# One output run of two rows, x's products in two 64x128 tiles, and M in eight 64x32 tiles

## The chip, the cores and the metric

The kernel runs on one core of a Trainium2 chip. The metric is the device time of one execution in microseconds. A core has the engines TensorE (PE), VectorE (DVE), ScalarE (ACT), GpSimd (POOL) and SyncE (SP), and 16 DMA engines. TensorE multiplies a loaded (stationary) matrix by a streamed (moving) one into PSUM, 8 banks of 512 fp32 numbers on each of 128 partitions; its array can be used as smaller tiles, each on its own rows and columns. SBUF is the working memory of 128 partitions.

## The reference

x has shape (128, 64, 512): 128 batches, 64 channels c, 512 times t. Each batch b has a subject s (one of 8 matrices W0, 64x64) and a condition (one of 200 matrices W1, 64x64).

```
x = x + einsum('bct,bcd->bdt', x, W0[subject])
x = x + einsum('bct,bcd->bdt', x, W1[condition])
```

All in fp32. Both steps together are one product: with M[b] = (I + W0[subject]) (I + W1[condition]), the output is M[b] transposed times x[b]. Input x and the output are 16.8 MB each; the gathered W1 matrices are 2.1 MB.

## The kernel before, in words

The kernel forms M for every batch and applies it to x once.

**Loads.** SP loads the conditions, then x in 16 DMAs of 1 MB (L110). A partition of `xy` holds, for one batch, two adjacent channels (j = 0, 1), 4 KB in a run; a slot is 4 batches, so a partition's row is (batch, channel pair). POOL builds the identity and, as soon as the conditions are there, issues one indirect DMA (L130) that gathers W1 of every batch, one batch in a partition. ACT loads W0 and the subjects.

**Preparation.** DVE clears `w0t_diag` in two parts, the second once the gather has been issued. PE turns W0 (L159), DVE adds the identity and writes `w0t`, twice, on either half of the partitions (L269). When the gather has landed DVE adds 1 to W1's diagonals (L276), and PE turns W1 in 8 turns of 8 transposes each (L171): 128x64 in, 64x128 out. DVE and ACT copy turns 0, 2, 4, 6 and 1, 3, 5, 7 from PSUM to `w1`, in two copies of 64x512 a turn (L222).

**Products that make M.** The 64 pairs of batches go in 8 groups of 8 pairs (16 batches, 4 slots). POOL picks the subject's matrix by a register and copies it into one of the two diagonal blocks of a 128x128 matrix of `w0t_diag` (L151, 16 copies a group). PE multiplies it by the pair's `w1` (L183), and DVE and ACT copy the group's M to `m`, four copies of 32x256 each (L236).

**x's products.** For a unit v (2 slots, 8 batches, 1 MB of x) PE makes 16 matmuls of 32x64 (L202): four row tiles (a batch each) by two column tiles (the slot), twice (the channel j), 512 columns each. Four banks hold a unit's result; there are six. DVE copies one slot's four pieces of 64x512 and ACT the other's (L242), over x in `xy`. Then SP writes the unit (L116): a partition holds one channel of a batch, so a run is 2 KB.

**Order.** It is written out by hand, each engine in its own list. PE: products of group g+1, then x's products of group g. DVE and ACT: copies of group g's x products, then the M copies of group g+2. SP: all loads, then the 16 outputs, each after its unit's eight copies.

Times name a matmul in fp32 as two records (two passes); a transpose is one. In the text a product is one instruction of the program.

Of the kernel before, what the change touches and what calls it, by code (L numbers as in the profile page):

```python
# [5 lines left out]
def bass_cond_residual_kernel(  # L6
# [15 lines left out]

    fp32 = mybir.dt.float32
# [5 lines left out]
    P = 2 * C  # L29
    J = 2  # L30
    Q = C // J
    PAIRS = B // 2
    SLOT = 4
    SLOTS = B // SLOT
    GROUP = 4
    GROUPS = SLOTS // GROUP
    GPAIRS = 2 * GROUP
    CHUNK = 2
    CHUNKS = SLOTS // CHUNK
    assert CHUNK == 2  # L40
    BANK = 512
    assert B == P and T == BANK and GPAIRS * C == BANK
    ROWS = S0 * C // P
    D_RING = 4
    M_RING = 2
    M_BANK = 6
    Y_BANKS = 6
    TURN = 8
    TURNS = C // TURN
    W1_RING = 3  # L50
    POOL = mybir.EngineType.Pool
    HALVES = [slice(0, C), slice(C, P)]

    x_view = x_dram.rearrange("(s b) (p j) t -> (b p) s (j t)", b=SLOT, j=J)
    out_view = out_dram.rearrange("(p h) c t -> (h c) p t", h=2)

    ctx = ExitStack()
    with ctx:  # L58
# [10 lines left out]
        w1 = sb("w1", [P, PAIRS, C], fp32)  # L69
        w0t_diag = sb("w0t_diag", [P, D_RING, GPAIRS, P], fp32)  # L70
        m = sb("m", [P, M_RING, GROUP, J, C], fp32)
# [11 lines left out]
        s_gather_sent = sem("s_gather_sent")  # L83
        s_zeros = sem("s_zeros")
        s_ident = sem("s_ident")
        s_d_clear = sem("s_d_clear")
# [6 lines left out]
        s_w0_diag = sem("s_w0_diag")  # L93
# [6 lines left out]
        s_x = [sem(f"s_x{n}") for n in range(CHUNKS)]  # L100
        s_out = [sem(f"s_out{n}") for n in range(CHUNKS)]

        block = ctx.enter_context(nc.Block())

        @block.sync
        def _(sp):
            sp.dma_start(cond[:, :], cond_dram.rearrange("(b o) -> b o", o=1)).then_inc(s_cond, 16)
            for n in range(CHUNKS):
                slots = slice(n * CHUNK, (n + 1) * CHUNK)
                sp.dma_start(xy[:, slots, :], x_view[:, slots, :]).then_inc(s_x[n], 16)  # L110
            for n in range(CHUNKS):

                sp.wait_ge(s_y_v, SLOT * (n + 1))
                sp.wait_ge(s_y_s, SLOT * (n + 1))
                pairs = slice(n * 2 * CHUNK, (n + 1) * 2 * CHUNK)
                sp.dma_start(out_view[:, pairs, :],  # L116
                             xy[:, n * CHUNK:(n + 1) * CHUNK, :].rearrange("q s (h t) -> q (s h) t", h=2)
                             ).then_inc(s_out[n], 16)
            for n in range(CHUNKS):
                sp.wait_ge(s_out[n], 16)  # L120

        @block.gpsimd
        def _(pool):
# [12 lines left out]
            pool.wait_ge(s_ident, 1)  # L136
            pool.wait_ge(s_gather, 16)
            pool.wait_ge(s_subjects, 16)
            pool.wait_ge(s_d_clear, 2)
            pool.wait_ge(s_w0t, 4)  # L140
            for g in range(GROUPS):
                if g >= D_RING:

                    pool.wait_ge(s_m_psum, g - D_RING + 1)
                first = g * 2 * GPAIRS
                _, picked = nc.values_load_multi_w_load_instructions(
                    subjects[0:1, first:first + 2 * GPAIRS], engines=(POOL,), min_val=0, max_val=S0 - 1,
                    skip_runtime_bounds_check_because="subjects index the 8 matrices")
                for n in range(2 * GPAIRS):
                    h, rows = n % 2, HALVES[n % 2]  # L150
                    nc.gpsimd.tensor_copy(w0t_diag[rows, g % D_RING, n // 2, h * C:(h + 1) * C],  # L151
                                          w0t[rows, bass.ds(picked[n] * C, C)]).then_inc(s_w0_diag, 1)

        @block.tensor
        def _(pe):
# [6 lines left out]

            pe.wait_ge(s_w1_plus, 1)
            for n in range(TURNS):
# [4 lines left out]
                for z in range(TURN):  # L169
                    bank = 2 * (n % W1_RING) + z // 4  # L170
# [4 lines left out]
            def products(g):  # L175

                pe.wait_ge(s_w0_diag, 2 * GPAIRS * (g + 1))
                if g >= M_RING:

                    pe.wait_ge(s_m_v, 4 * (g - M_RING + 1))  # L180
                    pe.wait_ge(s_m_s, 4 * (g - M_RING + 1))
# [4 lines left out]
                last.then_inc(s_m_psum, 1)  # L186

            def apply(g):

                pe.wait_ge(s_m_v, 4 * (g + 1))  # L190
                pe.wait_ge(s_m_s, 4 * (g + 1))
                for v in range(g * GROUP // 2, (g + 1) * GROUP // 2):
                    pe.wait_ge(s_x[v], 16)
                    for j in range(J):
                        for r in range(SLOT):
                            rows = slice(r * Q, (r + 1) * Q)
                            if j == 0 and SLOT * v + r >= Y_BANKS:

# [12 lines left out]
            for g in range(GROUPS):  # L211
                if g + 1 < GROUPS:
                    products(g + 1)
                apply(g)
# [96 lines left out]
```

## Time and profile before

| | |
|---|---|
| median of 3 runs | 99.78 us (99.7 to 100.39) |
| profiled execution | 100.29 us, of which the span 97.4 us |
| busy PE / PE loads / DVE / ACT / POOL | 69.0 / 37.3 / 67.6 / 54.8 / 31.8 us |
| busy mean of the 16 DMA engines | 98% or more until 75 us, 50 to 90% after |
| moved | 35.9 MB, 19.0 MB read, 16.8 MB written |

The span is what the trace covers; the rest of the execution's time, 2.9 us, lies around it. PE and PE loads overlap, and matmuls in different tiles overlap too, so that busy time says less of PE than the pace of its records.

### The profile page before, as it was taken

Reading aid. Unit: us, or ns where it says so; the run is one execution under the profiler, and the core shown is the slowest. Engines: PE = TensorE matmul, PEld = TensorE weight load, DVE = VectorE, ACT = ScalarE, POOL = GpSimd, SP = SyncE. Lnnn points to the kernel's source line nnn. Section 1 sums busy time; section 2 is a strip of 40 time slices with the busy share of each in tenths; the row PEclk is TensorE's granted clock in tenths of the full one; section 3 lists DMA queues with packets and bytes.
Section 4 is the critical chain, followed back from the end, with each engine's and each line's share of the span. In section 5 each row is a group of like instructions: output and inputs, shape, how many; then the busy total and the mean of one; then the engine's idle time right before and its main releaser. Section 6 shows DMA issues by size and latency. Waiting matters only on the chain.

```text
span 97.4 us, 2078 instructions
## 1 busy us (share of the span) xinstructions
PE 69.0 (71%) x708; PEld 37.3 (38%) x708; DVE 67.6 (69%) x111; ACT 54.8 (56%) x105; POOL 31.8 (33%) x135
## 2 busy tenths in 40 slices
PE   0400007997799999699699699979969969998000
PEld 0200006996782382265147138236414613322000
DVE  4293000588088889979979988997997997977900
ACT  2200000356277689759939938965992993955800
POOL 2400001888788788787758300000000000000000
PEclk9999999999999999999999999999999999999965
DMA  1999999999999999999999999999998984877975
GB/s 25 339 416 453 422 412 410 410 407 416 405 409 405 410 407 409 409 407 405 407 405 408 372 407 410 405 410 406 401 407 346 391 303 167 314 274 274 380 278 203
DMA packets 13243, 35.90 MB, mean 369 GB/s; under 512 B 689, under 2 KB 818, under 8 KB 13106
## 3 DMA queue, kind: packets, MB, share of 16 engines
q1 hardware_dynamic: 12944, 33.56, 88.5%
q0 software_dynamic: 144, 2.10, 5.0%
q10 hardware_dynamic: 146, 0.13, 0.4%
q8 instruction: 5, 0.08, 0.3%
q14 instruction: 4, 0.03, 0.1%
HBM read 19.01 MB, written 16.78 MB: 367 GB/s over the span
## 4 chain that ended last, share of the span: by engine, by line
PE 37%; DVE 34%; DMA 14%; issue 8%; DVEq 1%
PE psum L202 28%; DVE xy L242 21%; DVE m L236 12%; DMA w_rows<-in_L_cond_weights_dram,cond 12%; PE psum L171 8%; DMA cond<-in_itok_B_dram 3%; PE psum L183 2%; DVE w L222 1%; DVEq L58 1%; DVE w_rows L276 0%
## 5 line engine op out<-in xcount | busy, mean ns | idle before, releaser
L242 DVE COPY xy<-psum 64x512 f32<-64x512 f32 x64 | 43.8, 684 | 7.5 <-PE psum L202 5.8
L202 PE MATMUL psum<-xy,m 32*64 32x512 f32 x512 | 44.6, 600 | 5.1 <-DVE xy L242 5.1
L242 ACT COPY xy<-psum 64x512 f32<-64x512 f32 x64 | 37.2, 582 | 15.2 <-PE psum L202 13.8
L151 POOL COPY w0t_diag<-w0t 64x64 f32 x128 | 30.0, 234 | 19.9 <-issue 12.6
L202 PEld LDWEIGHTS psum<-xy,m 32*64 32x64 f32 x512 | 14.2, 130 | 29.9 <-DVE xy L242 18.4
L183 PEld LDWEIGHTS psum<-w,w0t_diag 128*128 128x128 f32 x128 | 14.8, 192 | 6.4 <-POOL w0t_diag L151 2.4
L183 PE MATMUL psum<-w,w0t_diag 128*128 128x64 f32 x128 | 15.7, 277 | 1.3 <-DVE w L222 1.3
L171 PE MATMUL psum<-ident,w_rows 128*64 128x128 f32 x64 | 8.5, 301 | 10.7 <-DVE w_rows L276 10.7
L236 DVE COPY m<-psum 32x256 f32<-32x256 f32 x32 | 13.3, 416 | 3.7 <-PE psum L183 2.8
L222 ACT COPY w<-psum 64x512 f32<-64x512 f32 x8 | 4.6, 578 | 17.3 <-PE psum L171 17.3
L236 ACT COPY m<-psum 32x256 f32<-32x256 f32 x32 | 11.7, 365 | 3.1 <-PE psum L183 2.4
L171 PEld LDWEIGHTS psum<-ident,w_rows 128*64 128x64 f32 x64 | 7.8, 155 | 11.7 <-DVE w_rows L276 11.2
L222 DVE COPY w<-psum 64x512 f32<-64x512 f32 x8 | 5.5, 683 | 3.6 <-PE psum L171 3.6
L276 DVE TENSOR_SCALAR w_rows<-w_rows 128x64 f32<-128x64 f32 x1 | 0.2, 225 | 6.7 <-DMA w_rows<-in_L_cond_weights_dram,cond 6.7
L159 PE MATMUL psum<-ident,w_rows 128*64 128x128 f32 x4 | 1.0, 414 | 3.5 <-DMA w_rows<-in_L_cond_weights_dram 3.5
L260 DVE MEMSET w0t_diag<- 128x2048 f32 x1 | 1.8, 1765 | 2.1 <-DMA w_rows<-in_L_cond_weights_dram,cond 2.1
L258 DVE MEMSET w0t_diag<- 128x2048 f32 x1 | 1.8, 1765 | 1.2 <-PEq L298 1.2
L222 ACT ACT_TABLE_LOAD x1 | 1.3, 1283 | 1.8 <-issue 1.8
L159 PEld LDWEIGHTS psum<-ident,w_rows 128*64 128x64 f32 x4 | 0.5, 157 | 3.6 <-issue 3.5
L130 POOL DMA_INDIRECT w_rows<-in_L_cond_weights_dram,cond x1 | 1.1, 1120 | 2.0 <-DMA cond<-in_itok_B_dram 2.0
L269 DVE TENSOR_TENSOR w0t<-psum,ident 64x256 f32<-64x256 f32 x4 | 1.4, 395 | 0.0
L126 POOL TENSOR_SCALAR_AFFINE_SELECT ident<-ident 128x128 f32<-128x128 f32 x1 | 0.3, 288 | 0.2 <-POOL ident L124 0.2
(5 smaller groups left out, 0.6 us busy)
## 6 DMA issues: line engine op xcount, KB each, us to landing
xy<-in_x_dram SPq DMA_DIRECT2D x16, 1024.0 KB, 19.5
out_dram<-xy SPq DMA_DIRECT2D x16, 1024.0 KB, 8.6
w_rows<-in_L_cond_weights_dram ACTq DMA_DIRECT2D x1, 128.0 KB, 2.6
cond<-in_itok_B_dram SPq DMA_DIRECT2D x1, 0.5 KB, 2.5
subjects<-in_itok_B_dram ACTq DMA_DIRECT2D x1, 0.5 KB
w_rows<-in_L_cond_weights_dram,cond POOLq DMA_INDIRECT x1, 11.5
```

The source lines that it names most:

```text
L130: nc.gpsimd.indirect_dma_start(out=w1_rows[:, :, :].rearrange("b d e -> b (d e)"), out_offset=None, in_=w1_dram.rearrange("s d e -> s (d e)"),
L151: nc.gpsimd.tensor_copy(w0t_diag[rows, g % D_RING, n // 2, h * C:(h + 1) * C], w0t[rows, bass.ds(picked[n] * C, C)]).then_inc(s_w0_diag, 1)
L159: last = nc.tensor.transpose(w0_psum[:, z * P:(z + 1) * P], w0_rows[:, z, :], ident[:, :])
L171: last = nc.tensor.transpose(psum[0:C, bank, (z % 4) * B:(z % 4 + 1) * B], w1_rows[:, :, n * TURN + z], ident[:, :])
L183: last = nc.tensor.matmul(psum[:, M_BANK + g % M_RING, k * C:(k + 1) * C], w0t_diag[:, g % D_RING, k, :], w1[:, g * GPAIRS + k, :], start= ...
L202: last = nc.tensor.matmul(psum[columns, (SLOT * v + r) % Y_BANKS, :], m[rows, g % M_RING, 2 * v + w - g * GROUP, j, :], xy[rows, 2 * v + w ...
L222: last = copy(w1[rows, :, n * TURN:(n + 1) * TURN], turned[:, h, :, :])
L236: copy(m[quarter, g % M_RING, :, j, :], of[:, a, :, :]).then_inc(done, 1)
L242: copy(xy[HALVES[r % 2], 2 * v + w, (r // 2) * T:(r // 2 + 1) * T], psum[HALVES[w], (SLOT * v + r) % Y_BANKS, :]).then_inc(done, 1)
L258: nc.vector.memset(w0t_diag[:, 0:2, :, :], 0.0).then_inc(s_d_clear, 1)
L260: nc.vector.memset(w0t_diag[:, 2:4, :, :], 0.0).then_inc(s_d_clear, 1)
L269: nc.vector.tensor_tensor(w0t[rows, :].rearrange("q (s j k y) -> q j s k y", s=S0, j=J, y=J)[:, j, :, :, :], turned[:, j, :, :, :], one[:, ...
```

## The change

- A slot's output is made in two 64x128 tiles: PE takes the rows of two batches (64 partitions) at once, and `m_diag` holds their M in a block-diagonal 64x128 stationary matrix whose other half is zero. A slot is 4 products of 512 columns, two for each of its two banks (L217), so a unit is 8 in place of 16. The even and the odd output channels come out in the two halves of the partitions and are copied so that `xy` holds two adjacent channels, 4 KB, in a run again, and `out_view` writes them so. A unit is still 2 slots, 1 MB.
- PSUM: three slots of two banks are in flight in place of six single banks, and a slot's copies are two for each of DVE and ACT (four in all, 64x512 as before).
- M: POOL (for the first two units DVE) copies the picked W0 matrix without a diagonal, `w0b`; PE makes M in 64x32 tiles, 16 products a unit (two row tiles, four column tiles, twice), in place of 4 a unit of 128x128.
- W1 is turned by matmuls with every other four columns of the identity, in two column tiles of 128x64: 128 products of 64 columns in place of 64 transposes of 128. A turn fills one bank and is copied in one copy of 128x512.
- The blocks of M are 1, 1, 2, 2, 2, 4 and 4 units. M's copies of a block go to `m_diag`, four an engine, of 32 x 128 numbers for each unit of the block.
- SP loads three slots of x, waits until the gather has been issued, and then loads the rest.
- DVE clears `m_diag` (128x4096) once, after the gather has been issued.

```diff
+    BLOCKS = [(0, 1), (1, 1), (2, 2), (4, 2), (6, 2), (8, 4), (12, 4)]
+    Y_RING = 3
-    out_view = out_dram.rearrange("(p h) c t -> (h c) p t", h=2)
+    out_view = out_dram.rearrange("(s b) (q i) t -> (b q) s (i t)", b=SLOT, i=J)
...
+            load(0, 2)
+            load(2, 1)
+
+            sp.wait_ge(s_gather_sent, 1)
+            load(3, 1)
+            for v in range(2, UNITS):
+                load(2 * v, 2)
...
-                    last = nc.tensor.transpose(psum[0:C, bank, (z % 4) * B:(z % 4 + 1) * B],
-                                               w1_rows[:, :, n * TURN + z], ident[:, :])
+                    for odd, rows in enumerate(HALVES):
+                        last = nc.tensor.matmul(psum[rows, n % W1_RING, z * C:(z + 1) * C],
+                                                w1_rows[:, :, n * TURN + z], of[:, odd, :, :],
+                                                start=True, stop=True)
...
-                for k in range(GPAIRS):
-                    last = nc.tensor.matmul(psum[:, M_BANK + g % M_RING, k * C:(k + 1) * C],
-                                            w0t_diag[:, g % D_RING, k, :], w1[:, g * GPAIRS + k, :],
-                                            start=True, stop=True)
+                if k >= 1:
+                    pe.wait_ge(s_m_v, SLOT * k)
+                    pe.wait_ge(s_m_s, SLOT * k)
+                for v in range(first, first + n):
+                    for j in range(J):
+                        for r in range(SLOT):
+                            for odd, rows in enumerate(HALVES):
+                                at = (v % M_COLUMNS * J + j) * C
+                                last = nc.tensor.matmul(psum[QUARTERS[r], M_BANK + odd, at:at + C],
+                                                        w0b[rows, v * SLOT + r, j * Q:(j + 1) * Q],
+                                                        w1[rows, v * SLOT + r, :], start=True, stop=True)
...
-                            for w, columns in enumerate(HALVES):
-                                last = nc.tensor.matmul(psum[columns, (SLOT * v + r) % Y_BANKS, :],
-                                                        m[rows, g % M_RING, 2 * v + w - g * GROUP, j, :],
-                                                        xy[rows, 2 * v + w, j * T:(j + 1) * T],
-                                                        start=j == 0, stop=j == J - 1)
+                    if s >= Y_RING:
+
+                        pe.wait_ge(s_y_v, 2 * (s - Y_RING + 1))
+                        pe.wait_ge(s_y_s, 2 * (s - Y_RING + 1))
+                    for j in range(J):
+                        for h, rows in enumerate(HALVES):
+                            last = nc.tensor.matmul(psum[:, 2 * (s % Y_RING) + h, :],
+                                                    m_diag[rows, odd, v % M_RING, j, :],
+                                                    xy[rows, s, j * T:(j + 1) * T],
+                                                    start=j == 0, stop=j == J - 1)
...
+            for n in range(EARLY * UNIT):
+                v, odd, r = n // UNIT, n // SLOT % 2, n % SLOT
+                nc.vector.tensor_copy(w0b[HALVES[odd], v * SLOT + r, :],
+                                      w0t[HALVES[odd], bass.ds(picked[n] * C, C)]).then_inc(s_w0b_early, 1)
```

PE's list before, from the turning of W1 through the first groups (`psum<-xy,m` are x's products, `psum<-w,w0t_diag` those that make M, each row's count at its end):

```order
L171 MATMUL psum<-ident,w_rows 64x128 x64
L183 MATMUL psum<-w,w0t_diag 128x64 x16
L202 MATMUL psum<-xy,m 64x512 x32
L183 MATMUL psum<-w,w0t_diag 128x64 x8
L202 MATMUL psum<-xy,m 64x512 x32
```

And the same place of PE's list in the changed kernel, with the last blocks:

```order
L178 MATMUL psum<-ident,w_rows 64x64 x128
L198 MATMUL psum<-w,w0b 32x64 x32
L217 MATMUL psum<-xy,m_diag 128x512 x8
L198 MATMUL psum<-w,w0b 32x64 x32
L217 MATMUL psum<-xy,m_diag 128x512 x8
```

Two units (a group of before) took 8 products for M and 32 for x; they take 32 for M and 16 for x now, and x's first products come after two blocks of 16.

DVE's list at the start, before:

```order
L258 MEMSET w0t_diag 128x2048
L260 MEMSET w0t_diag 128x2048
L269 TENSOR_TENSOR w0t<-psum,ident 64x8x32 x4
L276 TENSOR_SCALAR w_rows<-w_rows 128x64
L222 COPY w<-psum 64x64x8 x8
L236 COPY m<-psum 32x4x64 x8
```

and now, where the pair of an address instruction (ISA) and a copy comes 16 times before W1's diagonal (L300):

```order
L274 MEMSET m_diag 128x4096
L284 TENSOR_TENSOR w0t<-psum,ident 64x8x32 x4
L289 TENSOR_LOAD subjects
L295 ISA
L295 COPY w0b<-w0t 64x64
```

The addition to W1's diagonals, on which the turning of W1 waits, has moved behind these copies and behind the whole of the clearing.

## Rows read from the trace of the kernel before

**Rows 1.** The page, 40 slices, in tenths: PEclk granted clock, DMA busy share.

```profile
PEclk9999999999999999999999999999999999999965
DMA  1999999999999999999999999999998984877975
```

**Rows 2.** Chain of waits (start us, us, what), 84 us to the end.

```profile
83.63 2.67 PE psum L202 x26
...
87.06 2.67 PE psum L202 x24
...
89.75 0.68 DVE xy L242
```

**Rows 3.** Source view of the output DMAs, L116.

```profile
L116 SPq DMA_DIRECT2D out_dram<-xy x16: 372/373/4838, 33.8 to 92.6; - x16
...
DMA to landing us min/median/max: 4.3/8.6/19.4
```

**Rows 4.** Windows: one group of two units.

```profile
core 0: us, PE busy (x) PEld busy (x) DVE busy (x) ACT busy (x) POOL busy (x), PEclk, DMA share, GB/s
44.30:52.37 8.07, 7.30 (x81) 3.56 (x80) 7.12 (x13) 6.12 (x12) 5.93 (x26) 1.00 1.03 405
```

**Rows 5.** Timeline of PE loads (start us, us), first steps of L202.

```profile
28.89 0.24 PEld L202 LDWEIGHTS psum<-xy,m 32*64 32x64 f32 x16 [0.20 <-DVE m L236]
29.37 0.18 PEld L202 LDWEIGHTS psum<-xy,m 32*64 32x64 f32 x8 [0.25 <-issue]
```

**Rows 6.** Windows (span, busy PE, busy PE loads) on L183, products for M.

```profile
25.00:26.82 1.82, 1.75 (x16) 1.78 (x16) 1.00 1.02 405
```

**Rows 7.** Windows (columns of Rows 6) on L171, early and later turns of W1.

```profile
15.20:17.20 2.00, 1.94 (x10) 1.60 (x10) 1.00 1.03 414
18.90:19.78 0.88, 0.88 (x10) 0.88 (x9) 1.00 1.01 405
```

**Rows 8.** Windows (span, busy PE loads) just after a wait had ended.

```profile
85.07:85.11 0.04, 0.04 (x2) 1.00 1.24 461
```

**Rows 9.** Timeline of PE (start us, us) where L202 and L183 take turns.

```profile
42.37 2.00 PE L183 MATMUL psum<-w,w0t_diag 128*128 128x64 f32 x16
44.30 1.11 PE L202 MATMUL psum<-xy,m 32*64 32x512 f32 x16
```

**Rows 10.** Page, groups: line, engine, out<-in, count, busy, mean ns, idle before.

```profile
L242 DVE COPY xy<-psum 64x512 f32<-64x512 f32 x64 | 43.8, 684 | 7.5 <-PE psum L202 5.8
...
L236 DVE COPY m<-psum 32x256 f32<-32x256 f32 x32 | 13.3, 416 | 3.7 <-PE psum L183 2.8
...
L269 DVE TENSOR_TENSOR w0t<-psum,ident 64x256 f32<-64x256 f32 x4 | 1.4, 395 | 0.0
```

**Rows 11.** Chain of waits, start to the first x product.

```profile
3.49 11.46 DMA w_rows<-in_L_cond_weights_dram,cond
...
15.26 7.65 PE psum L171 x56
...
25.07 1.98 PE psum L183 x16
...
28.89 2.80 PE psum L202 x40
```

**Rows 12.** Timeline, the second clearing and the last ACT copies of W1.

```profile
5.10 1.76 DVE L260 MEMSET w0t_diag<- 128x2048 f32 x1 [2.10 <-DMA w_rows<-in_L_cond_weights_dram,cond]
...
23.80 1.17 ACT L222 COPY w<-psum 64x512 f32<-64x512 f32 x2 [0.58 <-PE psum L171]
```

**Rows 13.** DMA queues between 7.8 and 14.4 us (q0 is the gather).

```profile
q0 software_dynamic: 143, 2.10, 74.2%
q1 hardware_dynamic: 193, 0.73, 26.8%
```

**Rows 14.** Source view of POOL copies, L151 (ns min/median/max, first and last start).

```profile
L151 POOL COPY w0t_diag<-w0t x128: 230/236/245, 16.5 to 54.3; 64x64 f32 x128
```

**Rows 15.** DMA over a stretch of writes, 50 to 72 us.

```profile
DMA packets 4443, 8.86 MB, mean 403 GB/s; under 512 B 135, under 2 KB 135, under 8 KB 4439
```

More of the change, by code:

```diff
@@ L188, in apply, with products @@
[L188 to L193, printed above, removed]
+            def products(k):
+                first, n = BLOCKS[k]
+                if first + n <= EARLY:
+                    pe.wait_ge(s_w0b_early, UNIT * (first + n))
+                else:
+                    pe.wait_ge(s_w0b, UNIT * (first + n - EARLY))
+                if k >= 1:
+                    pe.wait_ge(s_m_v, SLOT * k)
+                    pe.wait_ge(s_m_s, SLOT * k)
+                for v in range(first, first + n):
@@ new lines, in products, with apply @@
+                last.then_inc(s_m_psum, 1)
+            def apply(k):
+                first, n = BLOCKS[k]
+                pe.wait_ge(s_m_v, SLOT * (k + 1))
+                pe.wait_ge(s_m_s, SLOT * (k + 1))
+                for s in range(2 * first, 2 * (first + n)):
+                    v, odd = s // 2, s % 2
+                    pe.wait_ge(s_x[v], 32 if v == 1 else 16)
+                    if s >= Y_RING:
[7 more added lines that the diff above has]
+                                                    start=j == 0, stop=j == J - 1)
@@ L210, in _ @@
             products(0)
[L211 to L214, printed above, removed]
+            for k in range(len(BLOCKS)):
+                if k + 1 < len(BLOCKS):
+                    products(k + 1)
+                apply(k)
         def copy_w1(eng, copy, done, n):
             eng.wait_ge(s_w1_turned, n + 1)
-            bank = 2 * (n % W1_RING)
-            turned = psum[0:C, bank:bank + 2, :].rearrange("q z (k p h) -> q h p (z k)", h=2, k=4)
@@ L238, in copy_y @@
[L238 to L254 removed]
+            part = slice(n * TURN // J, (n + 1) * TURN // J)
@@ new lines, in copy_w1, with copy_m @@
+            copy(w1[:, :, :].rearrange("q p (i e) -> q p i e", i=J)[:, :, :, part],
+                 psum[:, n % W1_RING, :].rearrange("q (y i p) -> q p i y", i=J, p=UNITS * SLOT)).then_inc(done, 1)
+        def copy_m(eng, copy, done, odd, k):
+            first, n = BLOCKS[k]
+            eng.wait_ge(s_m_psum, k + 1)
+            if first + n > M_RING:
+                eng.wait_ge(s_y_psum, 2 * (first + n - M_RING))
+            at = first % M_COLUMNS * J * C
+            for r, rows in enumerate(QUARTERS):
+                to = m_diag[rows, odd, first % M_RING:first % M_RING + n, :, :].rearrange(
+                    "q v j (i b e) -> q b (v j) i e", i=J, b=2)
+                copy(to[:, r % 2, :, :, :],
+                     psum[rows, M_BANK + odd, at:at + n * J * C].rearrange("q (w i e) -> q w i e", i=J, e=Q)
+                     ).then_inc(done, 1)
@@ new lines, in copy_y, with copies @@
+        def copy_y(eng, copy, done, i, s):
+            eng.wait_ge(s_y_psum, s + 1)
+            for h, rows in enumerate(HALVES):
+                copy(xy[rows, s, i * T:(i + 1) * T], psum[HALVES[i], 2 * (s % Y_RING) + h, :]).then_inc(done, 1)
+        def copies(eng, copy, w1_done, m_done, y_done, odd):
+            for n in range(odd, TURNS, 2):
+                copy_w1(eng, copy, w1_done, n)
+            eng.wait_ge(s_m_clear, 1)
+            copy_m(eng, copy, m_done, odd, 0)
+            copy_m(eng, copy, m_done, odd, 1)
+            for k, (first, n) in enumerate(BLOCKS):
+                for s in range(2 * first, 2 * (first + n)):
+                    copy_y(eng, copy, y_done, odd, s)
+                if k + 2 < len(BLOCKS):
+                    copy_m(eng, copy, m_done, odd, k + 2)
```

124 lines of the change are left out of this document (41 added, 83 removed).

## The prediction

> **What bounds the kernel now.** I read the page's slices first [rows 1]: the DMA engines are full until about 75 us and no longer, and PE's granted clock is full (2.4 GHz) until the last x product. So the last quarter is set by the engines, and the chain of waits there says by which [rows 2]: units follow each other every 3.43 us (83.63, 87.06) where no M is made, PE 2.67 us of it and one DVE copy. The last unit's copies start at 89.75, DVE's four take 2.83 us (each 0.684 and a gap of 0.03 [rows 10]), the last output is issued at 92.6 and lands after 4.3 us [rows 3]. From the last copy's end (92.58) to the span's end are 4.8 us. A group of two units with its products takes 8.07 us [rows 4], 4.04 a unit: DVE is busy 7.12 of it, so it is nearly as close to the bound as PE.
>
> How PE works is in the loads' timeline [rows 5]: eight tiles load and start together, and the next step follows after 0.43 to 0.48 us (28.89, 29.37). I take 0.429 us for 512 columns in one tile, in one pass of two; 16 products are 32 records in 8 tiles, four steps, 1.72 us of array for a unit. Four steps and a wait for copies in six banks make 3.43. The products for M cost 16 records in 1.82 us [rows 6], 0.112 each, and a group's 16 records with both changes of tile shape 1.93 us (42.37 to 44.30 [rows 9]).
>
> Before all that lies the gather: issued 3.49, landed 14.95, W1 turned from 15.26, products from 25.07, x's products from 28.89 [rows 11].
>
> **The change, part by part.** The sum follows PE from the gather on.
>
> *Gather.* While it moved its 2.10 MB, x took 0.73 MB of the same DMA engines [rows 13], at 0.41 MB/us 1.8 us. Now only 1.5 MB of x are queued before; but SP's next load is issued the moment the gather's issue is known (5.10, when DVE's second clearing starts [rows 12]), and from there x competes as before. Bounds: 0 and 1.8 us earlier; I take 0.6, near the low end, as x's three slots fill the queue until about 6.8 us and the rest follows at once. Landing 14.35.
>
> *DVE before it.* From 5.10: clearing 2 x 1.76 [rows 12], W0 1.46 for four, with its gap, then 16 picked copies of 64x64. A copy of 512 columns costs 0.684 and of 256 0.416 [rows 10], so 64 give 0.215, with a gap of 0.033 0.25; POOL's follow each other at 0.30 with all its gaps ((54.3 - 16.5) / 127 [rows 14]). 16 x 0.25 = 4.0: ready at 14.1, just under the gather. The cover is thin: at POOL's pace it is 14.9. Then the diagonal, 0.25: PE starts at 14.65 in place of 15.26.
>
> *Turning W1.* Before, a turn was 8 transposes of 128 columns at 0.109 (0.88 [rows 7]), the first 2.6 us at half that pace (10 records in 2.00 us [rows 7]) although the clock row shows full clock. Now it is 32 records of 64 columns in two column tiles, 16 a tile. A load of 64 columns is half of row 6's 0.112, a matmul of 64 half of 0.109; overlapped, 0.056 a record, 0.90 a turn, if the two tiles run side by side as eight do in [rows 5]. 8 x 0.90 + 1.3 for the slow start + 0.2 = 8.7 (8.5 before). If they do not, 15.9. ACT's last copies were 1.17 us in two [rows 12] and are one of 0.58. The products for M start at 14.65 + 8.7 + 0.03 + 0.58 + 0.07 = 24.0, 1.0 us earlier.
>
> *The first block.* The price of a small product is the main unknown. 16 products of a unit are 32 records in 8 tiles, 4 a tile at 0.056: 0.22 us of array. So what counts is how fast PE is fed. Nearest row: after a wait had ended, two products' loads start within 0.04 us [rows 8]; I take 0.036 each, 0.58 a unit. Lower bound the array, 0.014; upper bound the transposes' 0.109. 24.0 + 0.58 + 0.28 until the copies can start, four copies of 32x128 at 0.282 and 0.033 (1.26), then the second block's 0.58 and 0.25 to change: x's products start at 26.95. Block 1 waits for block 0's copies because both lie in the same two banks; that wait is in this sum.
> The Trainium skill, TensorE: Matmul & The Clock Gate, section Wait — 56ns, not 53.3ns?, says that a matmul costs about 62 ns of the sequencer's time when the hardware does not decode it, which binds for small ones. By it the sum would come to 104.7 in place of 99.1; the row shows two in 0.04 us and speaks for less.
>
> *x's products.* 8 products a unit, 16 records, but only two tiles of 64x128: 8 steps of 0.429, 3.43 us a unit where the array took 1.72. The other half of each stationary matrix is zero, so this is twice the array time for the same output. It is new on the path in full, and it takes the place of waits: three slots of two banks let PE run 5.1 us ahead of a copy, and a slot's two DVE copies take 1.43. Even behind M's copies for a block of four units (4 x 0.72 = 2.9) the bank comes free in time. 16 x 3.43 = 54.9 us.
>
> *Products for M, blocks 2 to 6.* 14 units, 224 products; 8 of each of the five blocks I count as queued behind x's products and free (16 loads start within 0.23 us in [rows 5]). 184 x 0.036 = 6.6, and 5 changes there and back at 0.35 (1.93 less 16 x 0.112 gives 0.14 from first product to x; with the step before it I take 0.35): 8.4 us. Per unit in the middle 3.43 + 0.6 = 4.0, as before; DVE's 2.87 + 0.9 = 3.8 lies just beneath it, and POOL's 16 copies for two units (16 x 0.30 = 4.8 [rows 14]) under both.
>
> *End.* 26.95 + 54.9 + 8.4 + 0.16 = 90.4. Only one slot is then to be copied: 0.03 + 1.43 in place of 2.83, 91.85. With 4.8 the span is 96.65, against 97.4. The 4 KB runs cost nothing and give nothing: writes in 2 KB runs moved 403 GB/s [rows 15] with the engines full, and from 75 us on they wait for outputs.
>
> The profiled execution had 100.29 with this span, 2.9 around it; the sum gives 99.55. The median is 0.5 lower: **99.1 us**. A measurement of this kernel can tell about 1% (98.8 to 100.8), so the forecast is no change, at its fast edge.
>
> **Rivals.**
> *Slow feeding, on the other side.* If a small matmul is issued at 0.055, half the transposes' 0.109 (each of those is a load and a matmul), the 216 products on the path (184 and the first two blocks' 32) cost 0.019 x 216 = 4.1 us more: 103.2. For it: no row shows a long stream of small ones, and 8 in flight would soon be used up. Against it: [rows 8]. It decides at 0.044 each, where the time passes 100.8.
> *Array pace.* If PE takes them as fast as queued loads start in [rows 5] (0.015), M's products cost 0.24 a unit: 3.9 us less over 184, 0.7 in the first blocks; DVE's 3.8 a unit then holds back about 1 us of it: 95.5. An earlier gather, up to 1.2 us, only counts if DVE's copies are faster too.
> *Column tiles one after the other* in W1's turning: 7.2 us more, 106. [rows 5] speak against it.
> *DVE's early copies late*, or no gain of the gather: 0.6 to 1 us more, 99.7 to 100.1.
> *The DMA engines as bound:* 15 outputs behind 19 MB of reads would end near 88, before the last unit; out.
>
> **Chances.** As forecast, within 1.2 us: 0.36 (faster by over 1% 0.15, within 1% 0.20, slower 0.01). Array pace: 0.24, faster. Slow feeding: 0.25 (slower 0.24, same 0.01). Column tiles: 0.08, slower. Late DVE: 0.07 (same 0.05, slower 0.02). In all faster 0.39, same 0.26, slower 0.35. Both signs hold most of it, so the forecast's own range is 97.9 to 100.3; the range for 8 in 10 is 95.2 to 104.2, from the array pace to slow feeding with a little more.
>
> **What would show it.** x's products: 16 records a unit at 0.21 us, 3.43 a unit, PE without waits. Products for M: two units within 1.1 us by my price, 0.5 by the array's, 1.8 by slow feeding. Turns of W1 every 0.90 us, not 1.8. Gather landing at 14.0 to 14.6 and DVE's last picked copy just before. One slot's copies after the last matmul. Wrong it is if DVE, not PE, ends the steps, or if two 64x128 tiles do not run together (then x's products alone would take 110 us).

## The result and the profile after

| | before | after |
|---|---|---|
| median | 100.09 us (99.7 to 104.27, 4 runs) | 107.63 us (107.07 to 108.14, 4 runs) |
| profiled execution, span | 100.29, 97.4 us | 107.07, 105.3 us |
| a turn of W1 (of 8), once under way | 0.88 us | 2.34 us |

The ratio is 1.0766 [1.0664, 1.0868]: slower by 7.7%, and outside the predicted range, which ended at 104.2. The ratio leaves out the one execution of 104.27 us of the kernel before, a slow one.

The chain of waits of the changed kernel (start us, us, what) answers to [rows 2, 11]:

```profile
3.46 10.29 DMA w_rows<-in_L_cond_weights_dram,cond
...
14.05 18.95 PE psum L178 x252
33.00 0.72 issue
33.73 0.55 PE psum L198 x29
...
35.71 0.68 PE psum L198 x32
36.39 4.90 PE psum L217 x16
41.29 0.79 PE psum L198 x53
42.08 3.63 PE psum L217 x16
...
71.39 27.69 PE psum L217 x128
99.08 0.02 issue
99.11 0.68 DVE xy L257
```

From 36.39 us to the last copy PE has the chain alone: every wait for DVE in the middle of the kernel has gone, as predicted. (The chain counts the records that it followed, x252; the kernel has 256 of them.) But L178, the turning of W1, has the chain for 18.95 us, where L171 had it for 7.65.

Laid side by side with [rows 2, 11], the stretches add up to the 7.9 us by which the span grew:

| stretch | before | after | difference |
|---|---|---|---|
| span's start to the turning | 15.26 | 14.05 | -1.21 |
| turning to the first product for M | 9.81 | 19.68 | **+9.87** |
| to the first x product | 3.82 | 2.66 | -1.16 |
| to PE's end (a copy follows at 89.75 and at 99.11) | 60.84 | 62.69 | +1.85 |
| to the span's end | 7.67 | 6.22 | -1.45 |

Windows on L178 (span, busy PE with records, busy loads with records, granted clock, DMA share, GB/s), the answer to [rows 7]: the first, the second and the last turn.

```profile
14.05:16.40 2.35, 2.35 (x32) 2.35 (x34) 1.00 1.03 422
16.40:18.74 2.34, 2.34 (x36) 2.34 (x36) 1.00 1.03 411
30.44:32.78 2.34, 2.34 (x36) 2.34 (x34) 1.00 1.03 406
```

A turn is 32 records, 16 in each column tile, and takes 2.34 us: 0.146 for a pair, or 0.073 a record. The pace is the same in the first turn as in the last, no wait is named, and in the last the clock is full (for the first see below). So this is not a slow start, and not a missing cover: it is a steady price of a record itself, its load and its matmul together. The page's group of these loads (busy us, mean ns, idle before) says which of the two to suspect:

```profile
L178 PEld LDWEIGHTS psum<-ident,w_rows 128*64 128x64 f32 x256 | 18.8, 251 | 10.0 <-DVE w_rows L300 10.0
```

One load of 64 columns is shown with 251 ns, 3.4 times as long as its share of the time, so more than one is open all the time. Loads overlap matmuls in a record, however, and a long load may only be one that waits. That has to be tried.

The small products and the clock, windows again (the first on L198, the others on all of PE):

```profile
41.29:42.08 0.79, 0.79 (x64) 0.63 (x64) 1.00 1.05 410
```

```profile
35.00:36.00 1.00, 0.29 (x24) 0.75 1.03 406
36.00:37.00 1.00, 1.00 (x33) 0.50 0.99 397
...
38.00:39.00 1.00, 1.00 (x6) 0.54 1.06 414
39.00:40.00 1.00, 1.00 (x8) 1.00 0.99 393
```

32 products for M (64 records) take 0.79 us, 0.025 each. And after 35 us the granted clock falls to 0.50, the lower level of 1.2 GHz, for 3.4 us; in [rows 1] it never fell before the end. x's first unit takes 4.90 us for this, the second 3.63.

One thing about the clock has to be known for all that follows. The trace's own record of the granted clock begins only at 18.43 us here and at 18.01 us in the kernel before; ahead of that the page and the windows print full clock because they have no record, not because it was read. In the kernel before, the pace of L171 changes at just that place: its transposes start every 0.213 us until 17.84 us and every 0.109 us from 18.36 on. L178 keeps 0.073 a record on both sides of 18.43.

### The profile page after: what moved, and what is told of

The parts are those of the page before. It is cut to its first block, busy times and chain, and to the rows that moved or that the text cites. A ratio compares the mean times of both kernels' runs of the same rounds, so it can differ in the third digit from the quotient of the medians.

```text
span 105.3 us, 2665 instructions
## 1 busy us (share of the span) xinstructions
PE 83.8 (80%) x1028; PEld 50.1 (48%) x1028; DVE 66.8 (63%) x118; ACT 51.9 (49%) x97; POOL 23.7 (22%) x119
## 4 chain that ended last, share of the span: by engine, by line
PE 79%; DMA 12%; DVE 2%; issue 1%; DVEq 1%; ACTq 0%; POOLq 0%
PE psum L217 55%; PE psum L178 18%; DMA w_rows<-in_L_cond_weights_dram,cond 10%; PE psum L198 6%; DMA subjects<-in_itok_B_dram 2%; DVE m_diag L249 1%; DVEq L64 1%; DVE xy L257 1%; ACTq L305 0%; DVE w_rows L300 0%; POOLq L149 0%; DVEq L241 0%
## 5 line engine op out<-in xcount | busy, mean ns | idle before, releaser
L217 PE MATMUL psum<-xy,m_diag 64*128 64x512 f32 x256 | 57.8, 604 | 0.0
L217 PEld LDWEIGHTS psum<-xy,m_diag 64*128 64x128 f32 x256 | 25.2, 191 | 28.4 <-issue 27.9
L178 PE MATMUL psum<-ident,w_rows 128*64 128x64 f32 x256 | 18.9, 320 | 9.5 <-DVE w_rows L300 9.5
L157 POOL COPY w0b<-w0t 64x64 f32 x112 | 21.9, 239 | 11.0 <-DMA w_rows<-in_L_cond_weights_dram,cond 9.4
L178 PEld LDWEIGHTS psum<-ident,w_rows 128*64 128x64 f32 x256 | 18.8, 251 | 10.0 <-DVE w_rows L300 10.0
L249 DVE COPY m_diag<-psum 32x256 f32<-32x256 f32 (+2 forms) x28 | 12.8, 458 | 4.4 <-PE psum L198 3.6
L249 ACT COPY m_diag<-psum 32x256 f32<-32x256 f32 (+2 forms) x28 | 11.0, 394 | 2.8 <-PE psum L198 2.2
L198 PEld LDWEIGHTS psum<-w,w0b 64*32 64x32 f32 x512 | 5.5, 108 | 6.3 <-issue 6.3
L198 PE MATMUL psum<-w,w0b 64*32 64x64 f32 x512 | 6.7, 230 | 2.2 <-DVE m_diag L249 1.5
L165 PE MATMUL psum<-ident,w_rows 128*64 128x128 f32 x4 | 1.0, 414 | 3.5 <-DMA w_rows<-in_L_cond_weights_dram 3.5
L165 PEld LDWEIGHTS psum<-ident,w_rows 128*64 128x64 f32 x4 | 0.5, 160 | 3.5 <-issue 3.5
L300 DVE TENSOR_SCALAR w_rows<-w_rows 128x64 f32<-128x64 f32 x1 | 0.2, 225 | 1.1 <-DMA w_rows<-in_L_cond_weights_dram,cond 1.1
```

The source lines that it names most:

```text
L157: nc.gpsimd.tensor_copy(w0b[HALVES[odd], v * SLOT + r, :], w0t[HALVES[odd], bass.ds(picked[n] * C, C)]).then_inc(s_w0b, 1)
L165: last = nc.tensor.transpose(w0_psum[:, z * P:(z + 1) * P], w0_rows[:, z, :], ident[:, :])
L178: last = nc.tensor.matmul(psum[rows, n % W1_RING, z * C:(z + 1) * C], w1_rows[:, :, n * TURN + z], of[:, odd, :, :], start=True, stop=True)
L198: last = nc.tensor.matmul(psum[QUARTERS[r], M_BANK + odd, at:at + C], w0b[rows, v * SLOT + r, j * Q:(j + 1) * Q], w1[rows, v * SLOT + r, : ...
L217: last = nc.tensor.matmul(psum[:, 2 * (s % Y_RING) + h, :], m_diag[rows, odd, v % M_RING, j, :], xy[rows, s, j * T:(j + 1) * T], start=j = ...
L249: copy(to[:, r % 2, :, :, :], psum[rows, M_BANK + odd, at:at + n * J * C].rearrange("q (w i e) -> q w i e", i=J, e=Q)).then_inc(done, 1)
```

## The experiments

**Theory L (loads).** The stationary matrix of the turning is `w1_rows[:, :, z]`: of each partition 64 numbers that lie 256 bytes apart. Such a load costs more than 0.056 us, and the two column tiles don't double its pace. Before, the same 64 numbers were loaded once, for a transpose of 128 columns that is one record (0.109), which hid the load. Now they are loaded four times: there are two products of 64 columns, one for each column tile, and a product in fp32 is two records, each with its own load (64 records of L171 have become 256 of L178). **Rivals:** the moving side (every other four columns of the identity) is slow; column tiles simply run one after the other; or the loss is elsewhere and the turning hides it. **Theory G** is about the clock: it falls because PE does little between 33 and 36 us. Where an experiment changes what is multiplied or where it lands, its text says so.

### The turning alone undone (e1), and again on another chip (e12)

```diff
-                    for odd, rows in enumerate(HALVES):
-                        last = nc.tensor.matmul(psum[rows, n % W1_RING, z * C:(z + 1) * C],
-                                                w1_rows[:, :, n * TURN + z], of[:, odd, :, :],
+                    bank = 2 * (n % W1_RING) + z // 4
+                    last = nc.tensor.transpose(psum[0:C, bank, (z % 4) * B:(z % 4 + 1) * B],
+                                               w1_rows[:, :, n * TURN + z], ident[:, :])
```

The copies of a turn are cut into four pieces for each, since the halves come out beside each other again. All else is as in the changed kernel.

> The changed kernel with W1 turned as before: 64 transposes of 128 columns, six banks, copies in pieces. Theory A (all of the loss is the turning of W1, 18.95 us for 256 records against 8.5): the turning takes 8.3 to 8.8 us again, the four-dimensional copies may add up to 1 us at its end, and the span falls from 105.3 by 9 to 10.5 us to 95 to 96.5 us, a little faster than the kernel before. Theory B (part of the loss is in x's products, 62.8 us from the first to the last against 60.8 before): the span stays above 98.

Measured: median 98.86 us (96.49 to 99.85) with 100.36 for the kernel before. The turning took 10.1 us (13.99 to 24.1). In the profiled execution x's first unit was the slow one, as its chain shows, and the clock beside it:

```profile
28.17 6.23 PE psum L216 x16
...
35.19 3.63 PE psum L216 x16
```

```profile
25.00:26.00 1.00, 0.46 (x32) 1.00 1.01 401
26.00:27.00 1.00, 0.00 (x0) 0.77 1.05 422
27.00:28.00 1.00, 0.51 (x32) 0.50 1.02 406
```

The mean granted clocks of the four executions were 0.949, 0.964, 0.948 and 0.995, and the last was the one of 96.49 us. So about 9 us of loss lie in the turning, and 1.6 to 3.4 us are at stake in the clock. The expectation of theory A was nearly right in kind and not in size: the turning took 10.1 us and not 8.3 to 8.8, since the transposes kept their half pace until 19.7 us, where the clock's record begins in this trace, and the span was 98.1. While the granted clock was 0.50 (26.54 to 33.37 us) a step of x's products took 0.85 us, and 0.43 after it: half the clock, half the pace.

> The kernel of e1_turn_back once more, on another chip, for its spread: its four runs had 96.49 at a mean clock of 0.995 and 98.08 to 99.85 at 0.948 to 0.964. Theory G (the low clock after W1's turning costs 1.5 to 3.5 us and comes in most runs): again most runs at 98 to 100 with a mean clock under 0.97, and a profile in which x's first unit takes 5 to 6.3 us. Rival (a disturbed chip that time): 96.3 to 97 in all.

Measured: median **96.81 us** (96.26 to 97.91), the kernel before 99.92 on the same chip; ratio **0.9784 [0.9675, 0.9894]**. Three of the four had a mean clock of 0.994 to 0.996, and the one of 97.91 us had 0.963: the clock seems to have fallen once in four here and three times in four in e1, which is neither theory G's "most runs" nor the rival's "in all". The profiled execution has a span of 94.5 us. Its chain, and PE's windows in the same pause:

```profile
26.70 0.46 PE psum L197 x29
27.16 3.63 PE psum L216 x16
30.79 0.79 PE psum L197 x53
...
60.83 27.69 PE psum L216 x128
88.52 0.02 issue
88.55 0.68 DVE xy L261
```

```profile
25.00:26.00 1.00, 0.17 (x24) 0.01 (x1) 0.58 (x3) 0.61 (x3) 0.94 (x6) 1.00 1.05 418
26.00:27.00 1.00, 0.30 (x32) 0.33 (x32) 0.56 (x2) 0.42 (x2) 0.94 (x7) 1.00 1.06 426
```

(Columns: busy PE, loads, DVE, ACT, POOL, clock.) PE is as idle as in e1, and the clock holds at 1.00. With it held, the kernel with everything but the new turning is 2.9 us shorter in span than the kernel before: x's first product comes 1.7 us earlier (27.16 against 28.89), what follows PE's end is 1.7 us shorter (5.98 against 7.67), and 0.5 of this is lost between (61.36 against 60.84).

### The moving side packed (e2)

```diff
+            nc.gpsimd.tensor_copy(sel[:, :, :].rearrange("q o (v r) -> q o v r", r=SLOT),
+                                  ident[:, :].rearrange("q (v o r) -> q o v r", o=2, r=SLOT)).then_inc(s_sel, 1)
...
-                                                w1_rows[:, :, n * TURN + z], of[:, odd, :, :],
+                                                w1_rows[:, :, n * TURN + z], sel[:, odd, :],
```

> The changed kernel, but the columns of the identity that are streamed lie packed in a tile of their own, 64 in a run in place of 16 runs of 4; the two column tiles and the loads stay as they are. Theory M (the moving operand's short runs set the 0.147 us of a record in each tile): a turn falls from 2.34 to about 0.9 to 1.0 us, the turning to about 8.7, the span to 95 to 97. Theory L (the loads of W1, 64 numbers 256 bytes apart, take 0.073 each and follow each other though the tiles are two): 2.34 a turn, span 105. Theory C (two 128x64 column tiles run one after the other): also 2.34.

Measured: median 108.27 us, ratio 1.0792 [1.0724, 1.0861]. The turning is one row of the chain:

```profile
14.52 18.90 PE psum L183 x256
```

18.90 us against 18.95: the moving side is not the cause, and theory M falls. Theories L and C both expected this.

### The loads packed (e3; W1 isn't turned)

```diff
-                                                w1_rows[:, :, n * TURN + z], of[:, odd, :, :],
+                                                w1_rows[:, n * TURN + z, :], of[:, odd, :, :],
```

The same instructions, but each load reads 64 neighbouring numbers.

> The changed kernel, but PE loads 64 neighbouring numbers of each partition of W1 in place of 64 that lie 256 bytes apart (so the W1 that it multiplies is not the turned one; the work and its order are the same). Theory L: a turn falls from 2.34 to 0.9 to 1.2 us, span about 95 to 97. Theories M and C: 2.34 a turn, span 105.

Measured in one execution: 101.40 us, span 99.6. Windows on L178, one early and two later:

```profile
14.01:16.04 2.03, 2.03 (x38) 2.03 (x40) 1.00 1.02 412
19.45:20.40 0.95, 0.95 (x40) 0.95 (x37) 1.00 1.03 410
20.40:21.33 0.93, 0.93 (x40) 0.93 (x36) 1.00 1.05 405
```

A turn takes 0.93 us from 19.45 us on, 0.058 a pair, where the prediction said 0.90. So the predicted pace was that of packed loads. And for them the two column tiles do run side by side: in one tile a record of 256 columns takes 0.217 us (the fillers of e7 below, six in 1.30), so one of 64 columns takes about 0.054, an estimate in proportion, and here a record starts every 0.029.

Before about 19.2 us a turn took twice that, 0.053 a record; the clock's record begins at 19.31 here. The strided loads of the changed kernel have no such step: 0.073 on both sides of 18.43, and in e4 the same on both sides of 19.02. So their price does not go with whatever halves PE's pace at the start, which fits numbers that are slow to be fetched and not an array that is slow. Why the spacing costs this much no run shows; only two spacings were tried, 4 and 256 bytes.

The span of 99.6 us is above the 95 to 97 that theory L expected. The kernel lost time in a way that no theory had named: PE stood still three times (0.43 us at 23.03, and the two below), and nothing the profile shows released it.

```profile
52.98 1.59 issue
54.57 0.34 PE psum L198 x15
...
62.94 2.30 issue
65.25 0.73 PE psum L198 x42
```

### One column tile at a time (e4)

```diff
-                        last = nc.tensor.matmul(psum[rows, n % W1_RING, z * C:(z + 1) * C],
+                        last = nc.tensor.matmul(psum[HALVES[z // 4], n % W1_RING, ((z % 4) * 2 + odd) * C:((z % 4) * 2 + odd + 1) * C],
```

Eight products in a row go to one column tile, then eight to the other; they land in other places, so M is another one.

> The changed kernel, but the first eight products of a turn go to one column tile and the next eight to the other, in place of alternating (so the pieces of W1 land in other places; the work is the same). Theory M (0.147 us in each tile, tiles side by side): most of a turn is serial now, 4 to 4.7 us a turn, span 118 to 124. Theory L and theory C (a shared path of 0.073 a record): 2.34 a turn, span 105.

Measured in one execution: 110.78 us. Window of one turn on L178:

```profile
17.00:19.86 2.86, 2.86 (x39) 2.86 (x37) 1.00 1.01 405
```

2.86 us for 32 records is 0.089 each with no neighbour to overlap with; by turns they cost 0.073. Had the tiles run fully side by side it would have been half of 0.089. No theory had expected this number (L and C 2.34 a turn, M 4 to 4.7), but it lies far nearer to L and C. The "serial tiles" rival is nearly true of these loads, and only of these.

### The new turning alone, in the kernel before (e6)

```diff
-                    bank = 2 * (n % W1_RING) + z // 4
-                    last = nc.tensor.transpose(psum[0:C, bank, (z % 4) * B:(z % 4 + 1) * B],
-                                               w1_rows[:, :, n * TURN + z], ident[:, :])
+                    for h, rows in enumerate(HALVES):
+                        last = nc.tensor.matmul(psum[rows, n % W1_RING, z * C:(z + 1) * C],
+                                                w1_rows[:, :, n * TURN + z], of[:, h, :],
```

> The kernel before with one part of the change alone: W1 is turned in two column tiles of 128x64 by every other column of the identity, 256 records in place of 64, each with a load of 64 numbers 256 bytes apart; one copy a turn. Theory L (the loads of both tiles share a path, 0.073 each from W1 as it lies): 2.34 us a turn, the turning 18.7 to 19 us, and the time goes from 100.4 up by 9 to 10.5, less about 0.6 for the single copy at the end: 109 to 110.5. Rival (in the changed kernel something else slows it, POOL's picks beside it or the held loads): 1 us or less.

Measured: 108.89 and 109.12 us in the two executions with a clock near 0.98 (two others took 112.85 and 113.37), against 99.93 for the kernel before. From the chain:

```profile
14.97 19.11 PE psum L172 x256
34.80 1.98 PE psum L185 x16
38.61 2.80 PE psum L204 x40
```

x's products start at 38.61 in place of 28.89. This one part costs 9 us alone; the rest of the change gives some of it back.

### Can the clock be held by filler work? (e7)

e1 with three matmuls of 256 columns ahead of each of the first two blocks of M; their results are overwritten.

```diff
+            def fill(bank, n):
+                for _ in range(n):
+                    nc.tensor.matmul(psum[:, bank, 0:4 * C], ident[:, :], w1_rows[:, 0:4, :], start=True, stop=True)
+            fill(M_BANK, 3)
...
+            fill(0, 3)
```

> W1 turned back to transposes as in e1_turn_back, and PE makes three matmuls of 256 columns that nobody reads in each of its two waits before x's first products. Theory G (the granted clock fell to half at 26.2 us because PE had little to do from 24 to 28, and x's first unit took 6.23 us in place of 3.6): the clock stays full, the span is 94.5 to 95.5 in every run, the time 96.3 to 97.3, 3 to 4% under the kernel before. Rival (the clock falls anyway, or the fillers delay the products): 98 to 99.5 as in e1_turn_back.

Measured: median 101.45 us (100.63 to 102.57), ratio 1.0141 [1.0081, 1.0200]. In the profiled execution the clock held, and x's first unit took 3.63 us; the mean clocks of the six lie between 0.965 and 0.995, so it may not have held in each. And the time is 2.6 us above e1's (98.86, on another chip) and 1.4% above the kernel before: neither theory G's 96.3 to 97.3 nor the rival's 98 to 99.5. The chain shows what took it (L225 are the fillers):

```profile
24.32 1.30 PE psum L225 x6
...
28.18 3.63 PE psum L216 x16
31.81 0.76 PE psum L197 x51
32.57 1.17 issue
...
63.27 0.62 PE psum L216
63.90 1.90 issue
65.80 27.75 PE psum L216 x127
```

The two stalls, 3.07 us, are more than the 2.6 us that the held clock saved in x's first unit (6.23 against 3.63). The span is 99.5 us, 1.4 longer than e1's: the rest of it, 0.9 us, lies in the third products and the last eight units, which the stalls interrupt. Both end 2.4 us after a packet of instructions began to move: the trace's list of DMA packets has one of 16 KB on the instruction queue (q8) at 31.28 and one at 63.37, and PE goes on at 33.74 and 65.80.

### Three questions at e7's size (e8, e9, e11), and fewer fillers (e10)

e8 has SP load x at once, as before:

```diff
-            load(2, 1)
-
-            sp.wait_ge(s_gather_sent, 1)
-            load(3, 1)
-            for v in range(2, UNITS):
+            for v in range(UNITS):
```

> e7_filled, but SP issues all loads of x at once, as before the change. Theory H (holding x back brought the gather forward by 1.2 us, from 14.95 to 13.75): the gather lands at 14.7 to 15.1 and the time is 1.0 to 1.3 us above e7_filled. Rival (the gather landed earlier by chance, or DVE's early copies hold the start anyway): within 0.4 us of it.

Measured: 101.66 us (99.62 to 102.59, 10 executions) against e7's 101.45 on the same chip: no loss to be seen in the time, where theory H expected 1.0 to 1.3 us. Three of the ten even took 99.62 to 100.62, less than the shortest of e7's six (100.63). The gather took 11.31 us from its issue, and 11.04 in e7. e7 is the slowest of ten profiled kernels that hold the loads (10.13 to 11.04, mean 10.46); the three that don't have 11.27 to 11.46. So this pair says 0.3 us, all the kernels together 0.9, and e8 alone does not settle it.

e9 writes runs of 2 KB from the same data (the rows land elsewhere):

```diff
-    out_view = out_dram.rearrange("(s b) (q i) t -> (b q) s (i t)", b=SLOT, i=J)
+    out_view = out_dram.rearrange("(p h) c t -> (h c) p t", h=2)
```

> e7_filled, but the output DMAs write runs of 2 KB through the old view of the output (so the rows land in other places; the bytes are the same). My prediction's theory (4 KB runs give nothing, since outputs wait for the engines): within 0.4 us of e7_filled. Rival (2 KB runs are slower by the 3% that their packets show, 0.084 us for 2 KB against 0.163 for 4 KB, and with x's products starting earlier the DMA engines are near their bound): 0.5 to 1.2 us slower.

Measured: 102.11 us (99.41 to 102.97, 4 executions) against e7's 101.45 (100.63 to 102.57). The median is 0.66 us higher, which is the rival's 0.5 to 1.2 and not the "within 0.4", but the spreads lie over each other. In the profiled executions x's first product comes 0.39 us later (28.57 against 28.18), before anything is written, and 0.30 more lies behind PE's end (6.26 against 5.96). So it is not shown that the runs of 4 KB give nothing; what they give is small, and this pair can't tell it from none.

e11 stops the loads of x from unit 8 on until the third block of M is made, so that the DMA engines are idle when the first stall comes:

```diff
+                if v == 8:
+                    sp.wait_ge(s_m_psum, 3)
```

> e7_filled, but SP holds back the loads of x's units 8 to 15 until the products of the third block are made (about 34 us), so that the DMA engines have nothing of x to move from about 28 to 35 us, while PE's first stall (32.6 to 33.7) lies there. Theory F with contention (the packets of instructions queue behind x's on the DMA engines): the first stall shrinks from 1.17 to under 0.5 us; the second, at 64 us, may stay; time 0.5 to 1.2 us under e7_filled. Rival (the fetch has its own latency, or it is no fetch): the first stall stays at 1.1 to 1.2 us and the time within 0.4 us of e7_filled.

e10 has three fillers of 512 columns in place of six of 256:

```diff
-                    nc.tensor.matmul(psum[:, bank, 0:4 * C], ident[:, :], w1_rows[:, 0:4, :], start=True, stop=True)
+                    nc.tensor.matmul(psum[:, bank, :], ident[:, :], w1_rows[:, 0:8, :], start=True, stop=True)
```

> e7_filled with three fillers of 512 columns in place of six of 256: about the same time on PE, three instructions fewer. In e7_filled PE stood still twice in the middle of a run of instructions without any semaphore (1.17 us after its 221st matmul record, 1.90 us after its 721st; 1.59 and 2.30 us after the 725th and the 850th in e3_packed_weights). Theory F (it waits for its own instructions, which come by DMA in packets of 16 KB, so the place is a place in the instruction stream): the stalls, if they come, come after the same number of records, 219 to 223 and 719 to 727, so after 57 of the 64 records of the third products and not after 51. Rival (a resource at that point of the program, such as POOL's copies or a bank): after the same instruction as before, 51 of 64. Time 99.5 to 101.5 by both.

Measured, on e12's chip: e11 100.90 us (99.47 to 101.48), e10 98.64 us (97.15 to 99.56), ratio of e10 0.9852 [0.9784, 0.9919]. Neither reaches e12's 96.81, which has no fillers: nothing of what they were meant to save was left over. Of e11's chain and then of e10's:

```profile
31.00 0.79 PE psum L199 x53
...
61.02 0.62 PE psum L218
61.65 3.27 issue
64.92 27.75 PE psum L218 x127
```

```profile
61.31 1.91 PE psum L216 x7
63.22 0.34 issue
63.55 26.35 PE psum L216 x121
```

In e11 the first stall is gone: its packet began at 28.26, in e7 at 31.28. But it can't be put down to the idle engines, since they were busy until 28.3 and the packet began before they were idle. The second stall is longer, 3.27 us, and its packet began at 62.67, 1.0 us after PE had already stopped. In e10 that packet began at 61.26 and the stall is 0.34.

All stalls have the same shape. PE stops after the same record in the kernels that share the list: record 221 in e7, e8 and e9, record 721 in these and in e11. In e10, whose list is 6 records shorter, the first stall didn't come, and the second again came after record 721, which is an instruction six records further on in the program. That is what theory F expected of it and the rival didn't: the place is counted in the list of instructions. And PE goes on 2.2 to 2.5 us after the packet's start (e3's three: 2.5, 2.40, 2.46). In e12, whose list is 12 records shorter, the packet at 30.34 began when 148 records had started, and PE started its 222nd record 2.99 us later without a stop. So all this fits a PE that runs out of instructions where a stretch of small ones is taken faster than they come; that it waits for them is inferred from the times, since the profile names no releaser. What starts a packet, and why it sometimes starts late, stays open: these kernels change the length of the list and the time at which PE reads it together.

## Why the prediction was wrong

**The step that failed** is the price of the turning: "A load of 64 columns is half of row 6's 0.112, a matmul of 64 half of 0.109; overlapped, 0.056 a record, 0.90 a turn, if the two tiles run side by side as eight do in [rows 5]." The loads of [rows 5, 6] read packed numbers; W1's read numbers 256 bytes apart. Packed, the price was right (e3: 0.93 a turn). As they are, a pair of loads costs 0.146 (after), and one with no neighbour 0.089 (e4). Eight turns are then 18.95 us in place of 8.7. The span came out 8.65 us above the sum: 10.25 more from this step, and 1.6 less from all others together. The row that knew was L171's own, 0.109 for one such load with a matmul of 128 columns [rows 7]: it is an upper bound for the load. A pair, one load in each tile, could cost up to 2 x 0.109, 28 us for all 128 pairs; the range should have held that, and it took its "serial" rival from the packed price (15.9) too.

The Trainium skill bears on this in two places. TensorE: Matmul & The Clock Gate, section LDWEIGHTS, gives a load's time by its columns alone. An estimate by that page's formula is 53 ns for 64 columns; the trace has 73 to 89 for a strided load with its matmul, so column count alone doesn't hold for these, while packed ones come near it (e3, 58 in each tile). SBUF — State Buffer, in the note on cachelines of its section Door 1: The DMA port swizzle, says that each access that goes to a new line of 16 bytes pays a penalty, and that fp32 numbers may stand four apart at most for free. By that rule packing the loads should help and the old spacing should not be cheap, and e3 (0.93 us a turn) agrees beside the changed kernel (2.34). The page names no price.

**Column tiles.** The rival had a chance of 0.08 and its time, 106, came nearest. That is in part luck. Its mechanism is half right: strided loads hardly overlap (0.073 in place of 0.089), packed ones do. But its price was the packed one taken twice, and the whole of it misses 2.34 a turn (it had 1.8).

**The first block and M's products.** Right in kind and too dear in the middle: 0.036 was the price taken, and 0.034 was measured in the first block (0.55 us for 16 products), but 0.025 in the later ones, 0.79 us for two units where the text said 1.1. The five later blocks took 5.19 us together in place of 8.4. From the first product to x's first it was 2.66 us against 2.95 by the same steps, although the second block ran partly at the low clock. Slow feeding fell: 0.055 did not come, and with it fell the sum of 104.7. The price of the array alone (0.014) fell too.

**x's products.** The mechanism as predicted: PE without waits, one slot's copies at the end. A unit takes 3.46 us in the last eight (27.69 us), 3.53 in pairs and 3.63 alone, against 3.43. All sixteen took 57.5 us in place of 54.9, of which 1.3 is the clock's. So from the first x product to PE's end the sum was off by only 0.8 us (62.7 in place of 63.5) because two errors, 3.2 less for M and 2.6 more for x, nearly cancel.

**The clock** was in no step. It cost 1.3 us in the first x unit (4.90 against 3.63). Theory G as first put, that the little work before it must bring it down, does not hold: e12 and e3 have the same pause and no fall. That more work there prevents the fall fits the profiled executions of e7, e10 and e11, but it isn't shown, since in e12 the clock held without. And the reading "the clock row shows full clock" for the half pace at the start was wrong: the trace has no record of the clock before 18.01 us, and the pace doubles where the record begins. The 1.3 us that the sum took for this start were not paid by the strided loads, which have one pace throughout.

**The start.** DVE's 16 picked copies took 2.2 us, not 4.0 (0.188 each at a pace of 0.135, while POOL's pace of 0.30 [rows 14] was not DVE's), and so did not bind. The gather landed at 13.75; I had taken 14.35, with 13.15 as the bound. Holding the loads is worth between 0.3 and 1.2 us of the gather, and 0.6 was within it; in the time of a whole execution e8 shows none of it. "The 4 KB runs cost nothing and give nothing" is neither shown nor refuted by e9.

## What to carry over

A price for a load belongs to how its numbers lie in memory as well as to how many there are: take it from a row that loads the same tensor the same way, and where that row is covered by longer work, use it as a bound and ask what uncovers it. Halving a matmul's columns to use two column tiles loads every stationary matrix twice, and putting fp32 products, two records each, in the place of transposes, one record, doubles the loads again; that pays only when loads are cheap beside what streams. And a part that loses can hide one that wins: with the turning left as it was, the rest of the change is faster than the kernel before by 2.2% in e12 (1.1 to 3.3) and by 1.5% in e1's medians, where the clock fell in three executions of four.

## What was not expected of the hardware

- Records (a load and a matmul of 64 columns) whose load reads 64 fp32 numbers 256 bytes apart: 0.089 us in one column tile, 0.073 each in two by turns, the same before and after the place at the start where packed ones (in two tiles) go from 0.053 to 0.029 each.
- Half pace for PE at the start, until the trace's record of the granted clock begins: 18.0 us in before, 18.2 in e12, 19.3 in e3, 19.7 in e1, 20.5 in e9, each time within 0.3 us of the change of pace (e3: 38 records in 2.03 us at 14 us, 40 in 0.95 at 19.5). The 1.00 that the page prints ahead of it is no reading. That the clock was at its lower level there is likely, since the step is the same factor of two as at 0.50 (0.85 us in place of 0.43, e1), but it is not recorded.
- The granted clock fell to 0.50 for 3.4 us (after, e4) or 6.8 us (e1, e2) after a stretch of little work, and did not fall after the same stretch in e3 and e12 (e1 and e12 are the same program).
- PE stood still for 0.34 to 3.27 us at fixed records of its list and went on 2.2 to 2.5 us after a 16 KB packet of instructions began. Twelve records of filler brought 3.07 us of it (e7), and six longer ones 0.34 (e10).
- The 0.7 us before M's first products (33.00 to 33.73) and the wait of the second block for the first one's copies (1.5 us, in which the clock fell) were not changed in any experiment: both blocks lie in the same two banks, and writing there before the copies are done would be a race.
